# Macaron block on one core: V projected in tiles of one token block by eight heads, with 512-column matmuls, and one down sum ahead of the turnings

## What is computed

```
x = x + 0.5 * ffn(layernorm(x))                  # w1 256x1024, gelu, w2 1024x256, biases
qkv = layernorm(x) @ w_qkv                       # 256 -> 3 * 1024, 16 heads of 64
sim = q @ k.T / 8 - slope[h] * |i - j|, causal   # per head, 512 x 512
x = x + softmax(sim) @ v @ w_out + b_out
x = x + 0.5 * ffn(layernorm(x))                  # the same weights again
```

## Time and profile before

| | |
|---|---|
| median of 3 runs | 2174.56 us (2174.05 to 2176.23) |
| profiled execution | 2174.91 us, span 2173.1 us |
| granted TensorE clock, mean | 0.995 |
| PE matmul busy | 2131.3 us, 98% |
| DVE, ACT, POOL busy | 69%, 57%, 48% |
| matmuls | 14720 |
| V's matmuls | 3 x 512, 128x256 |

### The profile page before, as it was taken

How to read it: one execution, slowest core, us unless ns; L and a number is a source line. 1 busy time by engine, 2 the same in 40 slices (tenths; PEclk the granted TensorE clock), 3 DMA queues, 4 the chain that set the end, 5 groups by cost and what they waited for, 6 DMA issues and landing times.

```text
span 2173.1 us, 41849 instructions
## 1 busy us (share of the span) xinstructions
PE 2131.3 (98%) x14720; PEld 1736.5 (80%) x14720; DVE 1501.5 (69%) x4029; ACT 1235.9 (57%) x3111; POOL 1052.8 (48%) x1770
## 2 busy tenths in 40 slices
PE   7999999999999999999999999999999999999997
PEld 5688787877878788787887878878787787878876
DVE  6766767667676676776768676676766767667664
ACT  4745746466464664736557365574646646466472
POOL 1743627446273553726537174372744627355371
PEclk9999999999999999999999999999999999999999
DMA  4422505234051341514315052250523405143151
GB/s 131 131 74 72 143 1 159 56 89 127 16 151 49 108 107 35 151 30 119 96 57 137 22 140 75 72 142 2 157 58 93 122 18 149 49 111 104 35 139 42
DMA packets 109986, 193.91 MB, mean 89 GB/s; under 512 B 34513, under 2 KB 53201, under 8 KB 109777
## 3 DMA queue, kind: packets, MB, share of 16 engines
q1 hardware_dynamic: 88816, 137.95, 22.6%
q0 software_dynamic: 20480, 52.47, 9.7%
q10 hardware_dynamic: 480, 0.82, 0.1%
HBM read 14.95 MB, written 8.39 MB: 11 GB/s over the span
## 4 chain that ended last, share of the span: by engine, by line
PE 87%; ACT 4%; POOL 4%; DVE 3%; issue 1%; SPq 1%; DMA 1%; DVEq 0%; POOLq 0%; ACTq 0%
PE ps L304 85%; POOL P L1005 3%; ACT P L641 2%; PE ps L358 2%; DVE P L842 1%; ACT L641 1%; SPq L247 1%; ACT qk L592 0%; DVE x L781 0%; DMA PT<-P 0%; DVE P L834 0%; DMA raw<-in_L_ffn_w 0%; POOL PT L247 0%; DVE gl L752 0%; DVE xn L775 0%
## 5 line engine op out<-in xcount | busy, mean ns | idle before, releaser
L1005 POOL TENSOR_SCALAR P<-P,rs 128x512 f32<-128x512 f32 (+3 forms) x1024 | 538.4, 543 | 440.5 <-DVE rs L825 437.2
L641 ACT ACTIVATE P<-P,mx 128x512 f32<-128x512 f32 (+3 forms) x1024 | 562.5, 553 | 194.9 <-DVE mx L834 194.7
L247 POOL DMA_DIRECT2D PT<-P x640 | 321.7, 508 | 238.6 <-DVE P L842 224.6
L842 DVE STREAM_TRANSPOSE P<-P 128x1792 f32<-128x1792 f32 (+1 forms) x256 | 374.2, 1486 | 12.7 <-POOL P L1005 12.1
L304 PE MATMUL ps<-PT,v 128*64 128x256 f32 (+1 forms) x3072 | 308.2, 350 | 10.7 <-DMA PT<-P 9.9
L304 PE MATMUL ps<-qk 64*128 64x512 f32 (+3 forms) x2048 | 310.9, 443 | 0.7 <-ACT qk L592 0.7
L304 PE MATMUL ps<-w2h,gh 128*128 128x256 f32 x1024 | 292.7, 286 | 0.7 <-DVE gl L752 0.7
L304 PEld LDWEIGHTS ps<-PT,v 128*64 128x64 f32 x3072 | 205.9, 138 | 107.8 <-issue 15.8
L304 PE MATMUL ps<-w2l,gh 128*128 128x256 f32 x1024 | 289.7, 283 | 0.0
L304 PE MATMUL ps<-w2h,gl 128*128 128x256 f32 x1024 | 289.6, 283 | 0.0
L592 ACT ACTIVATE qk<-ps 128x512 f32<-128x512 f32 x256 | 152.9, 597 | 230.8 <-PE ps L304 230.6
(11 more groups left out here) (85 smaller groups left out, 4389.0 us busy)
## 6 DMA issues: line engine op xcount, KB each, us to landing
PT<-P SPq DMA_DIRECT2D x1398, 80.0 KB, 2.6
PT<-P POOLq DMA_DIRECT2D x640, 80.0 KB, 2.7
x<-in_L_attn_x SPq DMA_DIRECT2D x16, 512.0 KB, 4.2
out_y<-x SPq DMA_DIRECT2D x15, 512.0 KB, 3.2
raw<-in_L_ffn_w SPq DMA_DIRECT2D x2, 512.0 KB, 5.9
raw<-in_L_ffn_w SPq DMA_DIRECT2D x1, 1024.0 KB, 8.8
rawq<-in_L_attn_w_qkv SPq DMA_DIRECT2D x1, 1024.0 KB, 6.6
rawk<-in_L_attn_w_qkv SPq DMA_DIRECT2D x1, 1024.0 KB, 8.7
```

The source lines that it names most:

```text
L247: e.dma_start(PT[c % 2][32 * m:32 * m + 32, g, :], P[c % 3][32 * g:32 * g + 32, m, :]).then_inc(landed.sem, 16)
L641: e.activation(p, p, ACT.Exp, bias=mx[:, r, i:i + 1], scale=-1.0, accum_out=sm[:, r, i:i + 1]).then_inc(s_ex.sem, 1)
L842: e.transpose(p, p).then_inc(s_tr.sem, 1)
L1005: e.tensor_scalar(p, p, rs[:, 2 * (c % 2) + h, i:i + 1], 1.0, ALU.mult, ALU.mult).then_inc(s_nz.sem, 1)
```

## The change

V's heads are grouped by eight instead of four. A tile ("v", g, t) holds one token block of group g: six matmuls of 512 columns fill the bank. There are two groups, still eight tiles a batch, and v's two buffers are 8 KB each. The space reserved at the bottom of SBUF for POOL's DMAs goes from 16 KB to 8 KB to make room. Three tiles instead of two run in the first part of a batch, then one each in steps 2 to 6, the last of group 0 in step 2. `values(b, c)` waits for the fourth tile of group c // 4. On DVE, in `begin`, the sum of down tile 1 moves ahead of the first turning.

```diff
-    at = [16512]
+    at = [8320]
...
-    QK, V, PP, PT_AT, GT = R, R + 8192, R + 16384, R + 47104, R + 67584
+    QK, V, PP, PT_AT, GT = R, R + 8192, R + 24576, R + 55296, R + 75776
...
-    v = [place(f"v{i}", [128, NT, 4, DH], F32, V + 4096 * i) for i in range(2)]
+    v = [place(f"v{i}", [128, NT, 8, DH], F32, V + 8192 * i) for i in range(2)]
...
-        return {6: [("v", 3, 0), ("v", 3, 1)], 7: []}.get(c, [("v", c // 2, c % 2)] if c >= 2 else [])
-
-    tiles = [("k", 0), ("q", 0), ("v", 0, 0), ("v", 0, 1)]
-    FIRST = 4
+        return {2: [("v", 0, 3)], 3: [("v", 1, 0)], 4: [("v", 1, 1)], 5: [("v", 1, 2)], 6: [("v", 1, 3)]}.get(c, [])
+
+    tiles = [("k", 0), ("q", 0), ("v", 0, 0), ("v", 0, 1), ("v", 0, 2)]
+    FIRST = 5
...
-                    _, g, u = tile
-                    gs = slice(2 * HD + g * 256, 2 * HD + g * 256 + 256)
-                    for j in range(2):
-                        ts = slice((2 * u + j) * 128, (2 * u + j) * 128 + 128)
-                        last = three(dst[:, j * 256:j * 256 + 256],
-                                     [(xth[:, k, ts], xtl[:, k, ts], wqh[:, k, gs], wql[:, k, gs])
-                                      for k in range(NK)])
+                    _, g, t = tile
+                    gs = slice(2 * HD + g * 512, 2 * HD + g * 512 + 512)
+                    ts = slice(t * 128, t * 128 + 128)
+                    last = three(dst, [(xth[:, k, ts], xtl[:, k, ts], wqh[:, k, gs], wql[:, k, gs])
+                                       for k in range(NK)])
...
-                e.wait_ge(s_pc.sem, s_pc.at((b, ("v", c // 2, 1))))
+                e.wait_ge(s_pc.sem, s_pc.at((b, ("v", c // 4, 3))))
...
-                                  v[(c // 2) % 2][:, j, 2 * (c % 2) + h, :], turned, n == 0, n == len(RUNS) - 1)
+                                  v[c // 4][:, j, 2 * (c % 4) + h, :], turned, n == 0, n == len(RUNS) - 1)
...
                 inverse(b, 0, 0)
-                turned(b, 0, 1)
                 if b > 0:
                     add3(b - 1, 1)
+                turned(b, 0, 1)
                 turned(b, 0, 0)
...
-    nc = bacc.Bacc("TRN2", target_bir_lowering=False, num_devices=1)
+    nc = bacc.Bacc("TRN2", target_bir_lowering=False, num_devices=1, dynamic_dma_scratch_size=8192)
```

More of the change, by code:

```diff
@@ L75, in build @@
     x3h = place("x3h", [128, NK, T], F32R, QK + 4096)
-    x3l = place("x3l", [128, NK, T], F32R, V + 4096)
+    x3l = place("x3l", [128, NK, T], F32R, V + 8192)
     o_at = (PP + 10240, PT_AT + 4096, PT_AT + 12288)
@@ L127, in build @@
     tiles_of = {b: tiles for b in B}
-    tiles_of[0] = tiles[:8]
+    tiles_of[0] = tiles[:9]
     for c in range(1, NC):
@@ L468, in begin @@
                     among[0] = (6, 7)
-                    proj_tile(b, tiles[3])
+                    for tile in tiles[3:FIRST]:
+                        proj_tile(b, tile)
                 proj_tile(b, ("k", 1))
@@ L578, in proj_copy @@
                 if tile[0] == "v":
[L579 to L585, removed]
+                    _, g, r = tile
+                    if b > 0:
+                        e.wait_ge(s_pv.sem, s_pv.at((b - 1, 4 * g + 3)))
+                    dst = v[g][:, r, :, :]
+                    src = src.rearrange("p (h d) -> p h d", h=8)
                 else:
@@ L651, in attention @@
                     exps(b, 0, 3)
-                    proj_copy(b, tiles[3])
+                    for tile in tiles[3:FIRST]:
+                        proj_copy(b, tile)
                 proj_copy(b, ("k", 1))
```

## The result

The changed kernel takes 2243.52 us (median of 4 runs, 2240.97 to 2244.77), the kernel before 2175.09 us (4 runs, 2174.05 to 2176.23). The ratio is 1.031, 95% interval 1.0298 to 1.0323: 3.1% slower. The forecast was 2237 us and 2.9%, the range 2212 to 2256. The profiled execution of the changed kernel took 2240.97 us, its span is 2239.2 us and its mean granted clock 0.985 (before: 2174.91, 2173.1 and 0.995).

The account below looks back on a forecast made before the run. PE, busy 98% of the span, was taken to bound the kernel. Six terms summed to +62.3 us on the profiled 2174.9 us: 2237.2, or 2236.9 against the median; forecast 2237 us, 2.9% slower, range 2212 to 2256 us.

Parts of the forecast that it names:

- Term 1: V's matmuls: 768 of 512 columns at 227.3 ns replace 1536 of 256 at 120.0 ns, -9.7 us.
- Term 2: Step 1: down tile 1's sum ahead of the turning frees PE's PSUM bank in time, 15 x 0.57 us, -8.6 us.
- Term 3: Step 2: values(b, 0) waits for ACT's copy of its last V tile, 1.12 us in 15 batches, +16.8 us.
- Term 4: Step 6: values(b, 4) waits for the bank of the first LayerNorm transpose, net 3.17 us in batches 1 to 14; +46.1 us altogether.
- Term 5: Three of four step-6 stalls in batches 1 to 14 make the granted clock fall, 1.69 us each, +17.7 us.
- Case (a): The new waits open but the clock stays full: 2219.5 us, chance 0.20.
- Case (b): The clock falls at every step-6 stall, and for longer: 2243 to 2255 us, chance 0.15.
- Term 6: Smaller SBUF space for POOL's DMAs: addresses move, nothing waits on it, 0 us.

Follow-up runs that it names:

- the experiment with filler: Changed kernel plus nine unused 512-column matmuls in the step-6 pause of batches 1 to 14, ahead of values(b, 4): 2222.24 us, ratio 1.0211.
- the version with cover: Changed kernel, values(b, 4) on bank 7, V tile (0, 3) first in step 2, up tile 6 before values(b, 6), second transpose on bank 4: 2172.83 us.
- the sum put back: Changed kernel, two V tiles in step 6, (0, 3) first in step 2, values(b, 4) on the free bank, down sum behind the first turning: 2187.11 us.

## Why the prediction was right, and where it was off

**Term 1, wide matmuls, -9.7: right in size.** Six wide products take 1.36 us (655.79 to 657.15), 12 narrow ones took 1.44. That x is the weight here made no difference. The Trainium skill's rule for the distance of two matmuls ("TensorE: Matmul & The Clock Gate", Back-to-back issue gap) would have 2.5 ns saved per pair; the traces have 12.7 (240.0 less 227.3), so they don't agree with it, and the measurement decides. What the term did not say is that the gain is only one where no wait stands behind it. With both waits undone all of it went into the wait for PT and the second transpose.

**Term 2, the sum, -8.6: right per batch.** 0.59 us a batch alone; in the last row of the table 64.57 becomes 63.99. Over the whole run the edit alone gave 6.2 us by the medians.

**Term 3, step 2, +16.8: right.** The wait is 1.10 us, 15 times. The table has 66.28 - 65.11 = 1.17 us for it.

**Term 4, the bank, +46.1: right.** The forecast had transposes and values 4.25 us apart, the trace has 4.12 (657.15 to 661.27). In the table: 11.36 less the 1.52 us by which one wide tile is shorter than two narrow ones is 9.84, and 13.03 is 3.19 us above this; the forecast was 3.17 net. That they meet so closely has some luck in it: the forecast had the stall 0.13 us too long, and the 0.21 us taken off for the old order were read in batch 3, whose distance in the kernel before is 11.48, 0.12 above the median. Batch 15's wait is 1.05 us, at 2170.99, where +1.2 was forecast. The step named the right link of the chain, the split's first half; the other end of its bounds (3.9 us, both halves) did not come.

**Term 5, the clock, +17.7: right in kind, a little low in size.** The forecast had three of four falls at 1.69 us, 10.5 falls; the trace has 10 of 14 at 1.9 us. The price came from one values product: it fits seven of the falls (1.3 to 1.7 us), and is too low for the three at 2.9 us, where the stretch at 0.50 does not end with that product. That the count came out as it did is partly luck, since the forecast took three of four from two pauses with different outcomes. Case (a), that the clock stays full, is refuted by the windows, and the experiment with filler shows what it would have given: a batch of 135.9 us. Case (b), a fall at every stall, is what the experiment with V tile (0, 3) first had, 14 of 14; the change itself did not. The Trainium skill (the same page, Why this matters for your kernels) warns only of longer idle gaps. The pauses of 2.61 and 2.60 us contradict it unless the transposes ahead of them count as idle too; the pause of 2.17 us at 76.12, which stands behind 512-column products and was followed by 0.50, contradicts it in either case. Its remark on transposes (PE-mode transpose), that they don't count as busy in the same way, would let the pause reach over all 4.12 us and would have had all 14 fall; 10 did, so the trace bears it out in part only.

**Term 6, buffers, 0: right**, by the experiment that had this edit alone.

**The sum, +62.3, against +66.1 in the profiled execution.** Without the clock, terms 1 to 4 gave batches 1 to 14 some 43.5 us (14/16 of -9.7, 14/15 of -8.6 and +16.8, and 44.4), and they cost 44.4. The 3.8 us that are missing are these 0.9 us and 1.4 of the clock (19.1 for 17.7) in these batches, and the rest is mainly another fall that the prediction didn't have, in batch 0. There the wait for PT was 2.17 us instead of the 2.03 of the earlier trace rows, and the first values product took 4.00 us:

```profile
76.12 4.00 PE L304 MATMUL ps<-PT,v 128*64 128x256 f32 x24 [2.17 <-DMA PT<-P]
```

The median of the four runs is another 2.6 us above the profiled one.

**Where the experiments' own expectations failed** is one cause, met in all that undid a wait or moved a tile: a wait was taken away, the others were taken to stay as they were, and the next one in line came up. Undoing both waits was expected to leave terms 1 and 2 as a gain and gave a loss of 0.2%. The wait for PT of pair 6, 0.96 us at 664.11, is not in the list of before, where PE came later. But the trace before shows how little room there was: less than 0.1 us in each of batches 1 to 14, so that PE and the spread of pair 6 arrived together there. The prediction's "Between these PE runs without a pause" was read from a list that such arrivals don't reach. Two experiments confirm this cause: with two V tiles back in step 6 the wait fell to almost nothing, and with 1.36 us of other work ahead of that product too. Of the scheme's 1.2 us a batch the version with cover still lacks 0.9, by the table in the rows "3 to 4" (0.3), "6 to 7" (13.02, where 13.92 - 1.36 = 12.56, so 0.5) and "0 to 1" (9.15, where 9.05 - 0.08 = 8.97, so 0.2). It was not tried to move the GELU with its tile, because its result lies where P of pair 6 still has to be read.

## What to carry to other kernels

When the number of tiles between two users of alternating buffers changes, follow the parity: the next user may land on a buffer whose reader is far behind on another engine, and here this cost 3.2 us in each of 14 batches, and 19 us more through the clock that fell behind it. Where one engine is busy 98%, look for the operands that arrive just in time before counting a saving: compare when each transfer lands with when its user starts, for a list of waits does not show the pairs that arrive together; a shorter step is worth its time only up to the first transfer behind it. Undo parts of a bundle one at a time: here the one small edit that cost nothing, a sum moved ahead of two turnings, was worth 0.3%, and the rest of the change hid it.

## What the runs showed of the hardware

- Whether the clock falls is not a matter of the pause's length alone. In the changed kernel pauses of 2.60 and 2.61 us with the same work around them were followed by 1.00 in batches 3, 7 and 11 (in batch 2 too, after 2.54 us) and by 0.50 in ten batches. From batch 3 on this repeats every four batches: none in 3, 7 and 11, 2.9 us in 4, 8 and 12, 1.7 us in 5, 9 and 13, 1.3 us in 6, 10 and 14. With the wait of step 2 gone, the pause (2.60 us, in batch 2 2.53) was followed by 0.50 in 14 of 14. The pause of 2.17 us at 76.12 was followed by 0.50, that of 2.03 us in the earlier trace rows was not. Two versions even have nearly equal pauses at the same place, before values(0, 0), with different outcomes: 3.54 us followed by 0.51 with two tiles in step 6, and 3.55 us followed by 1.00 with the sum put back, as shown with that experiment. What tips it stays open; nine matmuls in the pause, which left 0.46 to 0.54 us of it, prevented it in 14 of 14.
- A fall of the clock behind a pause cost 1.9 us on average here, so 126 matmuls whose results are not used made this kernel 21.3 us faster.
- Halving the space reserved for POOL's DMAs from 16 to 8 KB changed nothing that can be measured, with five transfers of 80 KB issued in 2.5 us (ratio 0.9987 to 1.0005).
